# A four-layer graph network on one core: edge-feature products made a layer earlier, and a spreading one-hot moved from ScalarE to VectorE

## The chip, the core and the metric

The kernel runs on one core of a Trainium2 chip. A core has five engines with an instruction stream each: TensorE (PE, with its weight loads as PEld), VectorE (DVE), ScalarE (ACT), GpSimd (POOL) and SyncE (SP), which here only issues DMAs. Semaphores order them. Sixteen DMA engines move data between the device's memory and the on-chip SBUF; PSUM, in 8 banks, takes what TensorE computes. The metric is device time in microseconds, lower is better.

## The reference, cut to what matters

6250 nodes of 256 features, 100,000 edges sorted by destination. Four layers follow one another: attention over edges (L0), a gather-add-ReLU-sum layer (L1), a weighted graph convolution (L2), and edge attention with edge features (L3). The change touches the edge stages of the last two.

```python
# L2 (the third layer); edge_row is the source here, edge_col the destination
support = x @ W
out = segment_sum(support[edge_col] * edge_val[:, None], edge_row) + b
# L3 (the last layer), 8 heads of 32
ep = edge_features @ We + be                  # [E, 64] @ [64, 32]
scores = einsum("ehd,ehd->eh", q[dst], k[src] + ep[:, None, :]) * 32 ** -0.5
scores = scores * edge_weights[:, None]
ex = exp(scores - segment_max(scores, dst)[dst])
attn = ex / segment_sum(ex, dst)[dst]
out = segment_sum(attn[:, :, None] * v[src], dst)
```

`ep` needs only inputs of the whole kernel: no layer ahead of the last one enters it.

## The kernel before

Edges are cut into tiles of 128, and one **step** is one edge tile against one tile of 128 destination nodes. There are 832 steps, handled in **groups** of 4 (208 of them). Tables made at the start hold for each step its destination tile `j` (`k.step_j`), its edge tile `i` (`k.step_i`), and for each lane its source row, destination within the tile (`k.dloc`) and weight. All work between engines is ordered by hand: every engine runs its own loop over the groups, and the order of the calls in that loop is the engine's order.

**Third layer, `gcn_edges`.** VectorE builds for each group a one-hot of destinations (`onehot`) and a matrix `same` of lanes with the same source, times the weight. PE multiplies them (`mix_group`, L1615), ScalarE copies the result to `mix` (L1643), PE multiplies that with the tile's `support` rows (`spread_group`, L1625), ScalarE copies the sums to `update` (L1650), and GpSimd scatters them with an adding indirect DMA (L1667) into four tables, one for each step of a group. A scatter waits for the one that a group earlier went to the same table. PE and ScalarE work one group ahead with the first half (`one_ahead`). PSUM banks 0 to 5 are in use; 6 and 7 are free.

**Last layer, `att_edges`.** Four groups make a **block**; there are 52. In iteration g the engines run:

- GpSimd: gathers the keys and values of group g + 4 (L2043), multiplies 5 of 8 heads of group g - 6 with the softmax weights (L2051).
- ScalarE: `spread_group(g + 2)`: |destination - lane| (L2072), then ReLU(1 - that) (L2077), which is the one-hot that spreads queries over edges, with `first` (L2076), its first column, once a block; `part` and `mark(g - 6)`: the one-hot for summing (L2083, L2090); `weigh(g - 6)`: the other 3 heads (L2098); once a block the exponentials (L2103, L2105).
- TensorE: `look_up(g + 1)`: the edge features times `We` (L2139, into bank `EP`), the queries by the one-hot `spread` (L2145, into two banks, `LOOK`); `add_up(g - 7)`: the sums of weighted values (L2159).
- VectorE: in this order `add_features(g)`: keys plus `EP` (L2231); first of four adds to the running sums of group g - 8 (L2306); `times_query(g)` (L2237); second add; `reduce_heads(g)` (L2241); third add; fourth add.
- SyncE: loads destinations (L2004, tile `drow`) and edge features (L1999, tile `feat`) four groups ahead.

Once a block the maximum over each destination's edges is found by scans across the block: VectorE L2253 and L2258 behind `add_features` of a block's first group, PE's transposes `ends` (L2168 to L2170), VectorE L2267 and L2272, and PE's `hand_back` (L2178 to L2183); L2253 waits for a transposition of the logits (`turn`, L2164) that PE does behind `add_up` in the block's last iteration. Every buffer between PE and VectorE is single: the look-ups of g + 1 wait for `times_query(g)`, L2139 of g + 1 for `add_features(g)`, and each sum for the add of the sum before it in the same bank.

## Time and profile before

| what | us |
|---|---|
| median of 3 runs (7069.73 to 7101.26) | 7084.02 |
| the profiled execution | 7118.91 |
| its span | 7117.1 |
| scatters of the third layer, first and last start | 3173.2 to 4744.2 |
| last layer's edges, first and last `add_features` | 5002.0 to 6623.3 |

Busy over the whole span: PE 4567.6 us (64%), DVE 4218.4 (59%), POOL 4152.5 (58%), ACT 2830.5 (40%). These shares are means over stages with different limits, so they tell little about either stage. In a line of a group, "idle" is the time that the engine sat idle just ahead of that instruction, with what ended it; a semaphore number used by several stages can carry the name of another stage's DMA.

### The profile page before, as it was taken

How to read it: one execution, taken by the hardware profiler on the slowest of the kernel's cores; microseconds unless marked ns; L12 is line 12 of the kernel's file. 1: busy time of each engine (PE TensorE's matmuls, PEld its weight loads, DVE VectorE, ACT ScalarE, POOL GpSimd, SP SyncE). 2: the span in 40 equal slices, each digit the busy share in tenths (PEclk: the TensorE clock that was granted, in tenths of full speed). 3: DMA queues.
4: the chain of work that ended last, by engine and by line, in shares of the span. 5: the costliest groups of instructions: out<-in, count | busy, mean ns of one | idle time of the engine just before them, and what ended most of it. 6: DMA issues, size and time to landing. Idle time of an engine off the chain costs nothing. (4 is left out here: it accounts for less than half of the span.)

```text
span 7117.1 us, 97234 instructions
## 1 busy us (share of the span) xinstructions
PE 4567.6 (64%) x17620; PEld 3413.6 (48%) x17621; DVE 4218.4 (59%) x10350; ACT 2830.5 (40%) x7829; POOL 4152.5 (58%) x3730
## 2 busy tenths in 40 slices
PE   7366666641455544775555555547578887888799
PEld 5234333320233333464444444436466666666688
DVE  4366666676555555674444444446587877887554
ACT  0133333344333333342222222223477777777543
POOL 1666666623666666238888888851566666666210
PEclk9666676775767777897777777769788888888899
DMA  6344444424555555227777777765565555565100
GB/s 200 104 106 107 108 110 107 108 85 145 178 173 173 171 176 171 77 73 105 103 105 103 104 103 105 104 134 187 163 175 168 170 172 170 170 179 171 50 32 28
DMA packets 644440, 920.30 MB, mean 129 GB/s; under 512 B 92783, under 2 KB 500943, under 8 KB 644272
## 3 DMA queue, kind: packets, MB, share of 16 engines
q0 software_dynamic: 277808, 587.53, 36.6%
q1 hardware_dynamic: 347024, 311.25, 15.0%
q10 hardware_dynamic: 19440, 19.79, 0.8%
q14 instruction: 124, 1.02, 0.0%
q8 instruction: 44, 0.72, 0.0%
HBM read 742.43 MB, written 175.77 MB: 129 GB/s over the span
## 5 line engine op out<-in xcount | busy, mean ns | idle before, releaser
L1667 POOL DMA_INDIRECT gcn<-c_update,c_target x832 | 1319.5, 1586 | 277.3 <-issue 217.1
L1306 PE MATMUL psum<-g_rows,g_onehot 128*128 x1664 | 622.9, 523 | 765.9 <-ACT g_rows L1221 346.8
L2043 POOL DMA_INDIRECT s_rows<-kv,s_idx x832 | 798.5, 960 | 536.5 <-PE psum L2159 252.4
L662 POOL DMA_INDIRECT e_rows<-hrow,e_idx x832 | 818.3, 983 | 484.8 <-issue 234.7
L1198 POOL DMA_INDIRECT g_rows<-x,g_idx x784 | 765.4, 976 | 423.8 <-issue 229.6
L1306 PEld LDWEIGHTS psum<-g_rows,g_onehot 128*128 128x128 f32 x1664 | 387.1, 254 | 1001.7 <-issue 948.4
L725 PE MATMUL psum<-e_rows,e_onehot 128*128 128x265 f32 x1664 | 653.1, 546 | 298.7 <-DVE acc L819 116.2
L1615 PE MATMUL psum<-c_same,c_onehot 128*128 128x128 f32 x1664 | 361.5, 385 | 650.9 <-DVEq L1593 650.9
L1615 PEld LDWEIGHTS psum<-c_same,c_onehot 128*128 128x128 f32 x1664 | 307.2, 276 | 752.7 <-DVEq L1593 415.0
L725 PEld LDWEIGHTS psum<-e_rows,e_onehot 128*128 128x128 f32 x1664 | 385.8, 258 | 508.4 <-issue 213.5
L1274 DVE TENSOR_TENSOR acc<-acc,psum 128x256 f32 x832 | 349.5, 420 | 419.3 <-issue 199.7
L1625 PE MATMUL psum<-support,c_mix 128*128 x1664 | 596.4, 524 | 0.0
L2145 PE MATMUL psum<-queries_sums,s_spread 128*128 x1664 | 535.4, 478 | 92.1 <-issue 65.3
L819 DVE TENSOR_TENSOR acc<-acc,psum 128x265 f32 x832 | 357.4, 430 | 327.0 <-issue 144.5
L2098 ACT ACTIVATE s_rows<-s_rows 128x32 f32<-128x32 f32 x2496 | 549.3, 306 | 2.3
L1221 ACT ACTIVATE g_rows<-g_rows (+1 forms) x196 | 207.1, 1057 | 806.2 <-DVE g_rows L1265 471.9
L2306 DVE SCALAR_TENSOR_TENSOR queries_sums<-queries_sums,keep,psum 128x264 f32 x832 | 400.4, 481 | 153.0 <-PE psum L2159 109.4
L1598 DVE TENSOR_TENSOR c_target<-c_shift,src_f 128x4 int32<-128x4 f32 x208 | 34.0, 163 | 768.5 <-POOLq L1666 689.3
L1625 PEld LDWEIGHTS psum<-support,c_mix 128*128 128x128 f32 x1664 | 448.0, 283 | 82.9
L2145 PEld LDWEIGHTS psum<-queries_sums,s_spread 128*128 128x128 f32 x1664 | 381.4, 241 | 164.0 <-issue 101.4
L2159 PE MATMUL psum<-s_rows,s_onehot 128*128 128x264 f32 x1664 | 435.0, 407 | 9.0 <-ACT s_onehot L2090 5.8
L1643 ACT COPY c_mix<-psum 128x512 f32<-128x512 f32 x208 | 121.8, 586 | 793.1 <-PE psum L1615 790.5
(358 smaller groups left out, 9245.0 us busy)
## 6 DMA issues: line engine op xcount, KB each, us to landing
g_attr<-in_edge_attr SPq DMA_DIRECT2D x196, 512.0 KB
c_srow<-rows_src SPq DMA_DIRECT2D x208, 256.0 KB
e_drow<-rows_dloc SPq DMA_DIRECT2D x208, 128.0 KB
s_drow<-rows_dloc SPq DMA_DIRECT2D x208, 128.0 KB
s_feat<-in_edge_feat SPq DMA_DIRECT2D x832, 32.0 KB
n_sums<-gcn SPq DMA_DIRECT2D x100, 256.0 KB
e_rows<-hrow,e_idx POOLq DMA_INDIRECT x832
gcn<-c_update,c_target POOLq DMA_INDIRECT x832
```

Of the source, the lines that this page charges most:

```text
L662: pool.indirect_dma_start(rows[u][:, s, 0:D + H], None, k.hrow, bass.IndirectOffsetOnAxis(ap=idx[u][:, s:s + 1], axis=0)).then_inc(gathere ...
L725: pe.matmul(k.psum[:, s, 0:W], onehot[q % 2][:, s, :], rows[u][:, q * GROUP + s, :], start=True, stop=True).then_inc(summed, 1)
L1198: pool.indirect_dma_start(rows[:, s, :], None, k.x1, bass.IndirectOffsetOnAxis(ap=idx[:, s:s + 1], axis=0)).then_inc(gathered[n % ROUND], 16)
L1306: pe.matmul(k.psum[:, s, 0:D], onehot[q % 2][:, s, :], rows[:, bass.ds(m[q % 2 * GROUP + s], 1), :].rearrange("p o d -> p (o d)"), start=T ...
L1615: ins = pe.matmul(k.psum[:, b, s * P:(s + 1) * P], onehot[b][:, s, :], same[b][:, s, :], start=True, stop=True)
L1625: ins = pe.matmul(k.psum[:, 2 + 2 * b + s // 2, (s % 2) * D:(s % 2 + 1) * D], mix[b][:, s * P:(s + 1) * P], k.support[:, bass.ds(j[q * GRO ...
L1667: pool.indirect_dma_start(k.gcn[a], bass.IndirectOffsetOnAxis(ap=target[q][:, a:a + 1], axis=0), update[q][:, a, :], None, compute_op=ALU. ...
L2043: pool.indirect_dma_start(rows[at.u][:, st, 0:2 * D], None, k.kv, bass.IndirectOffsetOnAxis(ap=idx[at.u][:, st:st + 1], axis=0)).then_inc( ...
L2098: ins = act.activation(mine, mine, ACT.Copy, scale=rows[at.u][:, s, 2 * D + h:2 * D + h + 1])
L2145: ins = pe.matmul(k.psum[:, LOOK + s // 2, (s % 2) * D:(s % 2 + 1) * D], spread[at.b][:, s * P:(s + 1) * P], k.q[:, bass.ds(j[s], 1), :].r ...
L2159: pe.matmul(k.psum[:, s, 0:W], onehot[at.b][:, s, :], rows[at.u][:, at.q * GROUP + s, D:SLOT], start=True, stop=True).then_inc(summed, 1)
L2306: dve.scalar_tensor_tensor(out=to, in0=to, scalar=k.keep[:, bass.ds(at.g * GROUP + s, 1)], in1=k.psum[:, s, 0:W], op0=ALU.mult, op1=ALU.ad ...
```

## The change

- The edge-feature product moves into `gcn_edges`. SyncE loads the features there, 4 DMAs a group; PE multiplies them with `We` behind `mix_group`, into PSUM banks 6 and 7; ScalarE copies the 128 x 128 result out behind its copy of `mix`; SyncE stores it, 64 KB a group, to a new table `k.edge_rows` in device memory, three groups behind.
- In `att_edges` SyncE loads one 64 KB piece of that table a group in place of four feature tiles, and ScalarE copies it into PSUM bank `EP` (`move_rows`), where `add_features` reads it as before. PE's matmuls L2139 are gone.
- `spread_group` moves from ScalarE to VectorE, as one comparison of `drow` with the lane number (bf16 in, fp32 out, 512 columns), with one of a single column for `first` once a block.
- `apart` is fp32 instead of bf16; some constants and semaphores go.

```diff
@@ gcn_edges: sync @@
+            def load_feat(g, q):
+                wait_if_any(sp, rows_done, g - RING + 1)
+                i = load_indices(nc, sp, k.step_i, g * GROUP, GROUP, EA_TILES - 1)
+                for s in range(GROUP):
+                    sp.dma_start(feat[q][0:EDGE_D, s, :], edge_feat[:, bass.ds(i[s] * P, P)]
+                                 ).then_inc(feat_landed[q], 16)
+
+            def store_rows(g, q):
+                sp.wait_ge(rows_copied, g + 1 + 2)
+                sp.dma_start(k.edge_rows[bass.ds(g, 1)].rearrange("o p n -> p (o n)"), edge_rows[q][:]
+                             ).then_inc(rows_stored[q], 16)
...
+                    load_feat(g, q)
+                    if not isinstance(it, int) or q >= BEHIND:
+                        store_rows(g - BEHIND, (q - BEHIND) % RING)
@@ gcn_edges: tensor, mix_group @@
+                pe.wait_ge(feat_landed[q], (it + 1) * (16 * GROUP))
+                pe.wait_ge(rows_copied, g + 1)
+                for s in range(GROUP):
+                    ins = pe.matmul(k.psum[:, ROWS_BANK + b, s * HEAD_D:(s + 1) * HEAD_D], feat[q][:, s, :], we_sb[:],
+                                    start=True, stop=True)
+                ins.then_inc(rows_done, 1)
@@ gcn_edges: scalar, copy_mix @@
+                act.wait_ge(rows_done, g + 1)
+                wait_if_any(act, rows_stored[q], it * 16)
+                act.copy(edge_rows[q][:], k.psum[:, ROWS_BANK + b, 0:GROUP * HEAD_D]).then_inc(rows_copied, 1)
@@ att_edges: sync @@
-            def load_feat(at):
-                wait_if_any(sp, ep_done, at.g - GB + 1)
-                i = load_indices(nc, sp, k.step_i, at.g * GROUP, GROUP, EA_TILES - 1)
-                for s in range(GROUP):
-                    sp.dma_start(feat[at.q][0:EK - 1, s, :], edge_attr[:, bass.ds(i[s] * P, P)]
-                                 ).then_inc(feat_landed[at.q], 16)
+            def load_rows(at):
+                wait_if_any(sp, rows_moved, at.g - GB + 1)
+                sp.dma_start(edge_rows[at.q][:], k.edge_rows[bass.ds(at.g, 1)].rearrange("o p n -> p (o n)")
+                             ).then_inc(rows_landed[at.q], 16)
@@ att_edges: scalar @@
-            def spread_group(at):
-                act.wait_ge(drow_landed[at.q], (at.n + 1) * 16)
-                wait_if_any(act, spread_ready, at.g)
-                act.activation(off[:], drow[at.q][:], ACT.Abs, bias=minus_lane[:, 0:1]).then_inc(off_ready, 1)
-                act.wait_ge(off_ready, at.g + 1)
-                wait_if_any(act, looked_up, at.g - 1)
-                if at.q == 0:
-                    act.activation(first[at.u][:], off[:, 0:1], ACT.Relu, bias=one[:, 0:1], scale=-1.0)
-                act.activation(spread[at.b][:], off[:], ACT.Relu, bias=one[:, 0:1], scale=-1.0
-                               ).then_inc(spread_ready, 1)
+            def move_rows(at):
+                act.wait_ge(rows_landed[at.q], (at.n + 1) * 16)
+                wait_if_any(act, ep_added, at.g)
+                act.copy(k.psum[:, EP, 0:GROUP * DH], edge_rows[at.q][:]).then_inc(rows_moved, 1)
...
-                    if Group(n, q, 2).live:
-                        spread_group(Group(n, q, 2))
...
                         weigh(at)
+                    if Group(n, q, 1).live:
+                        move_rows(Group(n, q, 1))
+                    if at.live:
                         mark(at)
@@ att_edges: tensor, look_up @@
-                pe.wait_ge(feat_landed[at.q], (at.n + 1) * (16 * GROUP))
-                wait_if_any(pe, ep_added, at.g)
-                for s in range(GROUP):
-                    ins = pe.matmul(k.psum[:, EP, s * DH:(s + 1) * DH], feat[at.q][:, s, :], we_sb[:],
-                                    start=True, stop=True)
-                ins.then_inc(ep_done, 1)
@@ att_edges: vector @@
+            def spread_group(at):
+                dve.wait_ge(drow_landed[at.q], (at.n + 1) * 16)
+                wait_if_any(dve, looked_up, at.g - 1)
+                if at.q == 0:
+                    dve.tensor_scalar(first[at.u][:], drow[at.q][:, 0:1], k.lane[:, 0:1], None, ALU.is_equal)
+                dve.tensor_scalar(spread[at.b][:], drow[at.q][:], k.lane[:, 0:1], None, ALU.is_equal
+                                  ).then_inc(spread_ready, 1)
...
             def add_features(at):
                 dve.wait_ge(gathered[at.slot], (at.turn + 1) * (16 * GROUP))
-                dve.wait_ge(ep_done, at.g + 1)
+                dve.wait_ge(rows_moved, at.g + 1)
...
                     if q == GB - 1 and at.live:
                         finish_logits(at)
+                    if Group(n, q, 2).live:
+                        spread_group(Group(n, q, 2))
                     if q == 0 and done.live:
                         link_steps(done)
                     add_step(sums, 3, j)
```

VectorE's stream in `att_edges`, the end of a block's last group, before: reduction of the heads, third add, `finish_logits`, fourth add.

```order
L2241 TENSOR_REDUCE s_logit<-s_rows 128x4x8
L2303 REGISTER_ALU
L2304 REGISTER_ALU
L2306 ISA
L2306 SCALAR_TENSOR_TENSOR queries_sums<-queries_sums,keep,psum 128x264
L2247 ISA
L2247 SCALAR_TENSOR_TENSOR s_logit<-s_logit,weight 128x128
```

The same place in the changed kernel.

```order
L2269 TENSOR_REDUCE s_logit<-s_rows 128x4x8
L2331 REGISTER_ALU
L2332 REGISTER_ALU
L2334 ISA
L2334 SCALAR_TENSOR_TENSOR queries_sums<-queries_sums,keep,psum 128x264
L2275 ISA
L2275 SCALAR_TENSOR_TENSOR s_logit<-s_logit,weight 128x128
L2248 TENSOR_SCALAR s_spread<-s_drow,lane 128x512
```

The comparison stands behind the third add (in the other groups with nothing between) and ahead of the fourth.

TensorE's stream at a block's first group, before: the end transposes, then `look_up` with its feature matmuls.

```order
L2170 MATMUL psum<-s_anti,s_local 2x128
L134 ISA
L134 TENSOR_LOAD step_j
L2136 ISA
L2139 MATMUL psum<-s_we,s_feat 128x32 x4
L2142 REGISTER_ALU
L2145 ISA
L2145 MATMUL psum<-queries_sums,s_spread 128x256
```

The same place in the changed kernel.

```order
L2191 MATMUL psum<-s_anti,s_local 2x128
L135 ISA
L135 TENSOR_LOAD step_j
L2163 REGISTER_ALU
L2166 ISA
L2166 MATMUL psum<-queries_sums,s_spread 128x256
```

The four feature matmuls and the wait for them are gone from between the transposes and the look-ups.

TensorE's stream in `gcn_edges` in the changed kernel, one group (`c_onehot` by `c_same` is the mixing, `c_feat` by `c_we` the new product, `c_mix` by `support` the spreading).

```order
L1648 MATMUL psum<-c_same,c_onehot 128x128 x4
L1654 MATMUL psum<-c_we,c_feat 128x32 x4
L1661 REGISTER_ALU
L1664 ISA
L1664 MATMUL psum<-support,c_mix 128x256
```

The new product stands between the mixing of group g + 1 and the spreading of group g; all else keeps its order.

## Rows read from the trace of the kernel before

**Rows 1.** The page's first line.

```profile
span 7117.1 us, 97234 instructions
```

**Rows 2.** Busy time in a stretch of the last, then of the third layer's edges.

```profile
core 0: us, PE busy (x) PEld busy (x) DVE busy (x) ACT busy (x) POOL busy (x), PEclk, DMA share, GB/s
5400.00:6600.00 1200.00, 975.02 (x4359) 785.56 (x4359) 967.83 (x1516) 908.52 (x3110) 796.18 (x778) 0.86 0.60 172
3400.00:4600.00 1200.00, 699.22 (x2535) 558.10 (x2533) 498.08 (x2376) 253.45 (x317) 1006.96 (x635) 0.74 0.74 104
```

**Rows 3.** Third layer's scatter and update copy: count, ns least/median/most, first to last start.

```profile
L1667 POOL DMA_INDIRECT gcn<-c_update,c_target x832: 1542/1550/2071, 3173.2 to 4744.2; - x167
L1650 ACT COPY c_update<-psum x208: 1012/1012/1012, 3171.3 to 4721.8; 128x1024 f32<-128x1024 f32 x104
...
who waited for it (us, times):
  POOL gcn L1667: 3.3, 11
```

**Rows 4.** Waits from 3400 to 4600 us (the last SyncE's own): total us, times, longest.

```profile
DVE c_target L1598 <- POOLq L1666: 526.3, 139, 4.8
...
POOL gcn L1667 <- DMA gcn<-c_update,c_target: 25.6, 84, 0.3
...
SPq L1562 <- DVEq L1593: 1095.0, 158, 8.0
```

**Rows 5.** Groups by line, 5400 to 6600 us, VectorE: count | busy, mean ns | idle.

```profile
L2306 DVE SCALAR_TENSOR_TENSOR queries_sums<-queries_sums,keep,psum 128x264 f32 x622 | 299.2, 481 | 110.1 <-PE psum L2159 76.2 <-issue 13.6 <-remote 12.5
L2231 DVE TENSOR_TENSOR s_rows<-s_rows,psum 128x1024 f32<-128x1024 f32 x156 | 190.1, 1218 | 64.4 <-DMA n_x<-in_x 43.4 <-issue 10.3
L2253 DVE TENSOR_TENSOR_SCAN s_local<-s_stop,psum 128x128 f32<-128x128 f32 x39 | 16.4, 421 | 54.4 <-remote 40.6 <-DMA s_far_gap<-rows_link 8.8 <-PE psum L2164 4.1
```

**Rows 6.** The same view: the feature matmuls, and ScalarE's two passes.

```profile
L2139 PE MATMUL psum<-s_we,s_feat 65*128 65x32 f32 x1244 | 190.0, 300 | 17.3 <-DVE s_rows L2231 11.2 <-issue 5.1
L2077 ACT ACTIVATE s_spread<-s_off,s_one 128x512 f32<-128x512 bf16 x156 | 112.0, 718 | 189.3 <-PE psum L2145 133.5 <-DMA n_x<-in_x 46.9 <-ACT s_off L2072 4.9
L2072 ACT ACTIVATE s_off<-s_drow,s_minus_lane 128x512 bf16<-128x512 bf16 x155 | 110.0, 710 | 3.0 <-DMA s_drow<-rows_dloc 3.0
```

**Rows 7.** Timeline of one block: start, length, engine, line, [idle before <- releaser].

```profile
5920.85 0.42 DVE L2253 TENSOR_TENSOR_SCAN s_local<-s_stop,psum 128x128 f32<-128x128 f32 x1 [2.21 <-remote]
...
5922.69 0.48 PE L2168 MATMUL psum<-ident,s_local 128*128 128x128 f32 x1 [4.37 <-issue]
...
5924.03 1.92 PE L2139 MATMUL psum<-s_we,s_feat 65*128 65x32 f32 x8
...
5925.76 3.36 PE L2145 MATMUL psum<-queries_sums,s_spread 128*128 x8
...
5929.82 0.49 DVE L2306 SCALAR_TENSOR_TENSOR queries_sums<-queries_sums,keep,psum 128x264 f32 x1 [0.48 <-PE psum L2159]
...
5930.83 0.48 PE L2178 MATMUL psum<-s_far_gap,s_select 4*128 4x128 f32 x2
...
5932.52 1.08 PE L2139 MATMUL psum<-s_we,s_feat 65*128 65x32 f32 x8
...
5933.44 1.97 PE L2145 MATMUL psum<-queries_sums,s_spread 128*128 x8
...
5935.24 1.94 PE L2159 MATMUL psum<-s_rows,s_onehot 128*128 128x264 f32 x8
...
5937.83 0.49 DVE L2306 SCALAR_TENSOR_TENSOR queries_sums<-queries_sums,keep,psum 128x264 f32 x1 [1.86 <-PE psum L2159]
```

**Rows 8.** Comparisons and one-source passes on VectorE: ns least/median/most; last row: busy, mean.

```profile
L786 DVE TENSOR_SCALAR e_spread<-e_drow,lane x208: 327/349/593, 202.8 to 1488.5; 128x512 bf16<-128x512 bf16 x104
L952 DVE TENSOR_SCALAR n_y<-n_y,n_mv,n_std x50: 399/410/1008, 2966.0 to 3143.0; 128x256 f32<-128x256 f32 x50
L952 DVE TENSOR_SCALAR n_y<-n_x,n_mv,n_std x50: 405/410/415, 6688.9 to 7073.6; 128x256 f32<-128x256 f32 x50
...
L922 DVE TENSOR_TENSOR c_onehot<-iota,dloc 128x512 f32<-128x512 f32 x208 | 144.6, 695 | 89.6 <-DVE c_target L1598 87.6 <-issue 1.0 <-PE psum L1615 0.4
```

68 lines of the change are left out of this document (40 added, 28 removed).

## The prediction

> **What bounds the kernel now.** First comes the page for the span, 7117.1 us [rows 1], then a table of two stretches, then for each which wait ends last. The change touches two stages, and [rows 2] has a stretch of each. In the third layer's edge stage (scatters from 3173.2 to 4744.2 us [rows 3]) GpSimd is busy 1007 of 1200 us, and what is left is the 0.3 us between two scatters. VectorE waits there for GpSimd (526.3 us at L1598), SyncE for VectorE (1095 us), and GpSimd only 0.3 us at a time for a landing [rows 4]. The copy that feeds the scatters is far ahead: the last of 208 starts at 4721.8 us, the last of 832 scatters at 4744.2, so the last group's first one is at about 4738.5 (the scatters' mean spacing is 1571 / 831 = 1.89 us), some 16 us behind the copy [rows 3]; "waited for it" is 3.3 us in all. This stage is a GpSimd stage.
>
> The last edge stage (5002 to 6660 us) has no such engine. From 5400 to 6600 us PE is busy 975, VectorE 968, ScalarE 909 and GpSimd 796 us of 1200 [rows 2]: four engines at 66 to 81%, chained. 39 blocks of 4 groups pass there, one in 30.8 us, of which VectorE is idle (1200 - 968) / 39 = 5.95. Nearly all of it stands in three rows [rows 5]: 110.1 us before the adds (L2306), for PE; 64.4 before L2231; 54.4 before the first scan L2253. L2231 waits for a gather or for the feature matmuls L2139. Its "DMA n_x" is a semaphore number with another stage's name; I read it as L2139, since GpSimd runs four groups ahead. ScalarE's own idle time is mostly a wait for PE's look-ups: 189.3 us before L2077 [rows 6]. So PE and VectorE bind each other, and ScalarE is a follower.
>
> [Rows 7] walk one block, t = 0 at 5920.85, the first scan. PE does the block's end transposes at 1.84, feature matmuls at 3.18 (1.92 us long at the low clock level), look-ups at 4.91; the add of the next group starts at 8.97 after 0.48 us of waiting. Hand-back L2178 is at 9.98, features at 11.67 (1.08 us), look-ups at 12.59, their sums at 14.39, the add at 16.98 after 1.86 us of waiting. Both waits have an L2139 in the chain ahead of them.
>
> **Part by part, third layer.** PE gets 4 feature matmuls a group (8 passes): 1.08 us at the high level, 1.92 at the low [rows 7], in the same order ahead of the spreading matmuls. PE is busy 699 of 1200 us there [rows 2] at 7.55 us a group, so 1.1 to 1.9 fit, and the 16 us by which the updates end up ahead cover them. ScalarE gets one 128-column copy, under the 0.72 us of a 512-column pass [rows 6], where it is busy 253 of 1200. SyncE gets five issues a group; it idles 1095 of 1200 us. Its store waits for a copy of three groups earlier, and behind it stands the next row load, needed four groups on: hidden. DMA work moves in: 256 packets of 512 B in, 128 out a group. The last stage moves 172 GB/s at a share of 0.60; here the share is 0.74 for 104 GB/s, and 192 KB more per 7.55 us are 25 GB/s, at the last stage's ratio a share of 0.09 (estimate). At 0.83 I take no stall. Only the start shows: two feature groups ahead of the first scatter, 2 x 1.9 us at the low level plus landing: **+5 us** (0 to +15). If the cover were gone the whole 1.1 to 1.9 us a group would count, over 200 us; nothing in the rows is near that.
>
> **Part by part, last stage, per block.**
> VectorE gets 4 comparisons of 512 columns, bf16 in and fp32 out, and one of one column. No row has that form. The nearest is L786, the same comparison with bf16 out: 0.327 / 0.349 / 0.593 us (least, median, most); the other end is a 512-column pass of two fp32 inputs, 0.695 [rows 8]. I take 0.42 (nearer L786, somewhat up for the wider output), 0.2 for the single column: 1.9 us a block. The order below shows each stands between third and fourth add, behind nothing new: its look-up wait is one that L2237 has already passed.
> ScalarE loses two 0.71 us passes a group [rows 6] and gets the copy back. It was a follower: nothing by itself, but VectorE no longer depends on its arrival at PE's look-ups. Its copy waits for L2231 of the group before, and behind it stands only the one-hot of a sum one group later; L2231 has it a whole group early.
> PE loses L2139, 190.0 us in this stretch; SyncE and the DMAs lose half their bytes and 3 of 4 issues, with nobody waiting for them.
>
> The walk again, without L2139 and with the new comparison. (1) Look-ups at 3.2 instead of 4.91, the add at 8.9: VectorE arrives there 0.42 later and no longer waits, so +0 in sum (8.97 before). (2) Sums end earlier, but the fourth needs VectorE's fourth add, so hand-back is at about 8.9; look-ups then need only L2237, at 10.9 instead of 12.59. From look-up to add it was 16.98 - 12.59 = 4.4; so the add could start at 15.3. VectorE arrives at 16.98 - 1.86 + 0.42 = 15.5. **-1.5**. (3) Two comparisons and the single column until the fourth group's L2237: **+0.6**. (4) From there to the next first scan the path is PE's (look-ups, sums, transposition of the logits); VectorE waits 2.21 us before that scan [rows 7], so the fourth comparison is hidden. Sum at an unchanged clock **-0.9 us** a block. I leave the 2.1 us that lie between the end of the first sum pair (5935.24 + 0.48) and the add that waits for it (5937.83) as they are; no row explains them.
>
> Two corrections. **Port:** VectorE's one-source passes are sometimes long beside GpSimd: L952 with a median of 410 has a 1008 in one node stage and stays under 416 in the last [rows 8], L786 with 349 has a 593. GpSimd is busy two thirds of this stage. +0.1 (0 to +0.6). The Trainium skill, "SBUF — State Buffer", "Who interferes with whom", says that a tensor_scalar in a two-port mode and a GpSimd instruction exclude each other for their whole length. By it a comparison that meets L2051 could wait most of a microsecond, and the sum would be near the slower rival's; the medians of rows 8 show that most do not.
> **Clock:** PE has a granted clock of 0.86 at a busy share of 0.81, and 0.74 at 0.58 [rows 2]. Without L2139 the share is (975 - 190) / (1200 - 20) = 0.67, on the line between them 0.79; time at 1.2 GHz goes from 28 to 43%, 4.5 us more a block. At that level look-ups and sums of a group need twice 3.9 us against some 6.1 of VectorE, about 0.2 us lost per us: up to 0.8. The low stretches now lie at the block's start, where PE waits anyway; I take +0.3 (0 to 1.3).
>
> Sum: -0.9 + 0.1 + 0.3 = -0.5 us a block, 52 blocks: -26; with +5: **-21 us**. The profiled execution has 7118.9 us (span 7117.1); it comes to 7098, and the median 7084 to **7063**.
>
> **Rivals.**
> *More comes free (6980).* If VectorE alone sets the pace, a block is 24.8 busy + 1.9 + about 2 us of waits for the scans, 28.7: -2.1 x 52 + 5 = -104. For: every engine loses work but VectorE. Against: step (4) stays PE's. 0.14.
> *PE's clock takes it back (7115).* The share of 1.2 GHz becomes that of the third layer, 0.52, 7 us more a block, +1.3: -0.9 + 0.1 + 1.3 = +0.5, x 52 + 5 = +31, 7115. The Trainium skill, "TensorE: Matmul & The Clock Gate", "HAM oscillation — how this bites in real kernels", says idle gaps between bursts throw the array back to the half rate; by that rule thinning PE's work is no gain. The trace bears it out as far as the lower share goes with the lower clock in rows 2, but PE's waits in front of look-ups stay far shorter than the one in front of the end transposes. 0.15.
> *VectorE becomes the bound (7136, slower).* Place: the comparison ahead of the fourth add, three times a block on the path. If it costs 0.69 rather than 0.42 and 0.2 of port each, that is 3 x 0.47 = +1.4: -0.5 + 1.4 = +0.9, x 52 + 5 = +52. It decides from about 0.6 us each. For: no row of this form, VectorE already at 81%. Against: L786. 0.18.
> *The third layer pays.* A scatter waits for the one a group before on the same table; more packets could delay landings beyond that. 0.1 us a scatter would be +83 us, 7146. Rows 4 show no wait over 0.3. 0.04.
> *It does not do what it says:* the feature matmuls would still be on the last stage's path in another dress, as ScalarE's copy, if that came late. It would give about 7084 + 5. 0.03, inside the forecast's range.
>
> **How the numbers follow.** The forecast has 0.46, with its own range 7025 to 7100. A measurement of this kernel tells about 0.5% (35 us) from no change. Faster by more, below 7049: 0.14 and 0.20 of the forecast's. Slower by more, above 7119: 0.18, 0.04 and a little of the clock's. Rest 0.43. Range 6990 to 7130: it leaves out the ends of the first and third rival.
>
> **What would show it.** Right: no wait for PE before the addition of features to the keys; the wait before the second add of a block (1.86) nearly gone; the comparison at 0.35 to 0.45; GpSimd's spacing of 1.89 kept in the third layer; block 30.3. Wrong: a comparison over 0.6; granted clock under 0.78 in the last stage; scatters that wait for landings; or the idle before the first scan growing by what was saved.

## The result

The changed kernel took 6914.76 us, median of 5 runs (6888.0 to 6928.39), beside 7083.2 us for the kernel before in the same comparison: a ratio of 0.9756, with a 95% interval of 0.9735 to 0.9776. That is 168 us less. The forecast was 21 us less, and the lower end of its range was 6990. The sign was right, and the time lies below the range.

The profiled execution of the changed kernel has 6888.0 us (span 6886.3). Its two stretches, a table with the columns of [rows 2]:

```profile
5200.00:6400.00 1200.00, 915.50 (x3524) 684.15 (x3524) 1144.92 (x1935) 858.57 (x3300) 912.37 (x873) 0.88 0.63 182
3400.00:4600.00 1200.00, 897.11 (x3846) 760.75 (x3845) 506.07 (x2412) 297.80 (x480) 1004.78 (x642) 0.71 0.83 131
```

VectorE went from 968 to 1145 of 1200 us in the last stage: it now has 1.25 us of idle time in a block of 27.3 us, where it had 5.95 in 30.8. The groups of the same stretch answer to [rows 5] (busy, mean ns | idle time before):

```profile
L2334 DVE SCALAR_TENSOR_TENSOR queries_sums<-queries_sums,keep,psum 128x264 f32 x704 | 334.2, 475 | 36.4 <-PE psum L2180 16.2 <-issue 8.1 <-remote 5.6
L2259 DVE TENSOR_TENSOR s_rows<-s_rows,psum 128x1024 f32<-128x1024 f32 x176 | 212.5, 1207 | 8.0 <-issue 8.0
L2248 DVE TENSOR_SCALAR s_spread<-s_drow,lane 128x512 f32<-128x512 bf16 x175 | 90.7, 518 | 0.0
L2281 DVE TENSOR_TENSOR_SCAN s_local<-s_stop,psum 128x128 f32<-128x128 f32 x44 | 18.5, 420 | 10.6 <-PE psum L2185 8.2 <-issue 2.3
```

All three waits of [rows 5] are much shorter: 110.1 us in 39 blocks became 36.4 in 44, 64.4 became 8.0, and 54.4 became 10.6. The new comparison has a mean of 0.518 us. The scatters of the third layer, the comparison and the addition of features over the whole run (ns least/median/most, first to last start), against [rows 3] and, for the addition, the table of times ahead of the prediction:

```profile
L1712 POOL DMA_INDIRECT gcn<-c_update,c_target x832: 1542/1551/2063, 3150.4 to 4705.1; - x167
```

```profile
L2248 DVE TENSOR_SCALAR s_spread<-s_drow,lane x208: 464/476/1969, 4956.1 to 6389.4; 128x512 f32<-128x512 bf16 x104
```

```profile
L2259 DVE TENSOR_TENSOR s_rows<-s_rows,psum x208: 1183/1203/1223, 4963.0 to 6395.5; 128x1024 f32<-128x1024 f32 x104
```

From the first to the last scatter it is 1554.7 us instead of 1571.0, and from the first to the last addition of features 1432.5 instead of 1621.3. The pair of profiles is 230.8 us apart: 22.8 of it lie ahead of the scatters, in code that the change leaves alone, 16.3 among the scatters, 188.8 in the last stage, 3.0 behind it. The medians are 168 apart, so some 60 us are the difference of two single executions.

### The profile page after: what moved, and what is told of

Read it like the earlier page. It is cut to its first block and busy times, and to the rows that moved or that the text cites. A ratio compares the mean times of both kernels' runs of the same rounds, so it can differ in the third digit from the quotient of the medians.

```text
span 6886.3 us, 98886 instructions
## 1 busy us (share of the span) xinstructions
PE 4592.4 (67%) x17620; PEld 3430.3 (50%) x17621; DVE 4278.0 (62%) x10609; ACT 2679.4 (39%) x7777; POOL 4159.0 (60%) x3730
## 5 line engine op out<-in xcount | busy, mean ns | idle before, releaser
L1712 POOL DMA_INDIRECT gcn<-c_update,c_target x832 | 1303.3, 1566 | 271.4 <-issue 235.4
L2077 POOL DMA_INDIRECT s_rows<-kv,s_idx x832 | 817.4, 982 | 341.6 <-issue 221.7
L1664 PEld LDWEIGHTS psum<-support,c_mix 128*128 128x128 f32 x1664 | 427.3, 269 | 76.0
L676 ACT ACTIVATE e_rows<-e_rows 128x64 f32<-128x64 f32 x1664 | 407.5, 333 | 16.4 <-issue 15.4
```

What stands on the lines that cost most here:

```text
L676: ins = act.activation(rows[u][:, s, at], rows[u][:, s, at], ACT.Copy, scale=rows[u][:, s, D + h:D + h + 1])
L1664: ins = pe.matmul(k.psum[:, 2 + 2 * b + s // 2, (s % 2) * D:(s % 2 + 1) * D], mix[b][:, s * P:(s + 1) * P], k.support[:, bass.ds(j[q * GRO ...
L1712: pool.indirect_dma_start(k.gcn[a], bass.IndirectOffsetOnAxis(ap=target[q][:, a:a + 1], axis=0), update[q][:, a, :], None, compute_op=ALU. ...
L2077: pool.indirect_dma_start(rows[at.u][:, st, 0:2 * D], None, k.kv, bass.IndirectOffsetOnAxis(ap=idx[at.u][:, st:st + 1], axis=0)).then_inc( ...
```

## Two levels of one kernel

The experiments came in five sets, each with the kernel before run beside it, and the kernel before did not take the same time in all of them. It took 6558 and 6562 us in the first two sets, and 7080, 7078 and 7136 us in the three later ones; beside the result it had 7083. The text calls these the quick and the slow level. Kernels of one set share the level, so ratios are compared within a level only. The number of the chip does not tell which it is: chip 8 had both. A profile of the kernel before from the quick level shows what is different.

> The kernel before, unchanged, for its profile beside the ones of this call. The first four experiments ran on a chip on which the kernel before takes 6558 us and whose profiles have no wait named remote, while the first pair of profiles (7119 and 6888 us) had such waits, some 2 us long, around VectorE, GpSimd and ScalarE in the last stage. Theory L (signals between engines come late on the first chip): this run has a last stage of about 1450 us on such a chip and over 1600 us on one like the first. Theory N (the chips differ in DMA or clock only): the idle times of VectorE have the same causes on both, and no remote.

It took 6569.11 us, in one run. From the first to the last addition of features it needs 1470.2 us (4606.5 to 6076.7), the changed kernel beside it 1421.7. What SyncE waits for, first at the slow level (kernel before, 5200 to 6200 us; us in total, times, longest):

```profile
SPq L134 <- PE psum L2139: 53.3, 17, 4.6
SPq L134 <- DMA n_x<-in_x: 13.7, 6, 4.4
```

and then at the quick level (the same kernel, 5000 to 6000 us):

```profile
SPq L134 <- PE psum L2139: 305.6, 70, 6.3
```

SyncE, which only issues DMAs, has 67 of 1000 us to spare at the slow level and 306 at the quick one. The difference shows in its own register instructions for the feature loads, slow level first (ns least/median/most):

```profile
L1999 SPq FUSED_REGOPS  x832: 3/37/1477, 4993.2 to 6593.7; - x167
```

```profile
L1999 SPq FUSED_REGOPS  x832: 37/37/47, 4597.2 to 6042.3; - x167
```

At the slow level an instruction of 0.037 us takes up to 1.477 us at times. There, too, signals of PE come late. The timeline of the kernel before at the slow level has the product of a group on PE and the addition of features that waits for it:

```profile
5474.71 1.05 PE L2139 MATMUL psum<-s_we,s_feat 65*128 65x32 f32 x8
...
5484.32 1.22 DVE L2231 TENSOR_TENSOR s_rows<-s_rows,psum 128x1024 f32<-128x1024 f32 x1 [5.64 <-DMA n_x<-in_x]
```

The product ended at 5475.76 us, and the addition starts 8.6 us later, after 5.64 us of waiting. The keys that it also needs had landed 19 us before. ("DMA n_x" is another stage's name on the semaphore of the product, as the prediction says.) In the stretch of [rows 5] 15 of 156 of these waits are longer than 1 us. They make 41.8 of the 64.4 us, and each ends 2.4 to 8.6 us after the product's end on PE. The first scan is alike: its 16 waits named "remote" (40.6 us), a name that the profile gives where it finds no release, end 1.7 to 3.9 us after PE's transposition of the logits, and 4 us or more after the landing of the tables that it also needs. This is theory L. In the quick level's profile, from 4800 to 6000 us, no wait before the addition is over 1 us, the longest of the first scan for PE is 0.3 us, and "remote" is not there at all.

## The experiments

The ratio is to the kernel before of the same set. The changed kernel itself was not run again in the later slow sets: its 0.9756 is from the set of the result, and differences from it at the slow level go across sets.

| kernel | level | median us | ratio | 95% interval |
|---|---|---|---|---|
| changed | slow | 6914.76 | 0.9756 | 0.9735 to 0.9776 |
| changed | quick | 6501.89 | 0.9902 | 0.9885 to 0.9919 |
| features only | quick | 6496.17 | 0.9906 | 0.9889 to 0.9922 |
| features only | slow | 6911.54 | 0.9759 | 0.9742 to 0.9775 |
| spread only | quick | 6556.79 | 0.9998 | 0.9988 to 1.0008 |
| spread only | slow | 7092.45 | 1.0019 | 1.0009 to 1.0029 |
| comparison twice | quick | 6592.38 | 1.0051 | 1.0034 to 1.0068 |
| PE product back, late | quick | 6662.01 | 1.0160 | 1.0143 to 1.0177 |
| PE product back, early | quick | 6549.28 | 0.9973 | 0.9961 to 0.9984 |
| PE product back, early | slow | 7024.59 | 0.9930 | 0.9910 to 0.9949 |
| loads back on SyncE | slow | 7082.81 | 1.0011 | 1.0001 to 1.0020 |
| loads back, fixed address | slow | 6991.20 | 0.9803 | 0.9783 to 0.9824 |
| before, fixed address | slow | 7105.26 | 0.9953 | 0.9934 to 0.9971 |
| shared spread | quick | 6495.80 | 0.9897 | 0.9880 to 0.9914 |
| before, PE late | slow | 7073.59 | 0.9990 | 0.9978 to 1.0002 |
| changed, PE late | slow | 6953.44 | 0.9825 | 0.9808 to 0.9841 |
| rows from SBUF | slow | 6902.88 | 0.9751 | 0.9735 to 0.9768 |
| no GpSimd multiply | slow | 6921.05 | 0.9770 | 0.9754 to 0.9787 |

### Which of the two moves

Features only: `spread_group` goes back to ScalarE, in the two passes it had before.

```diff
-            def spread_group(at):
-                dve.wait_ge(drow_landed[at.q], (at.n + 1) * 16)
...
+            def spread_group(at):
+                act.wait_ge(drow_landed[at.q], (at.n + 1) * 16)
+                wait_if_any(act, spread_ready, at.g)
+                act.activation(off[:], drow[at.q][:], ACT.Abs, bias=minus_lane[:, 0:1]).then_inc(off_ready, 1)
...
```

> The changed kernel, but ScalarE keeps the spreading one-hot of the last layer in its two passes, at the place it had before; VectorE's comparison is gone. So of the two moves only that of the edge-feature product is made. Theory A (the move of the product off PE made the gain; the comparison is a pure cost to a VectorE that is now busy 95% of the last stage): VectorE loses 4 x 0.52 + 0.2 = 2.3 us a block, but ScalarE comes to 19.5 + 4 x 1.42 = 25.2 us a block, against 27.3 for the block now, so a block takes 25.5 to 26.5 and the time is 6830 to 6880. Theory B (the gain came from VectorE having the one-hot ready for PE, which ScalarE brought late): most of the gain goes again, time 7000 to 7080. Theory C (each half brings about half): 6970 to 7010.

> The kernel with the product's move alone (ScalarE keeps the one-hot), once more, for a call in which the kernel before takes 7080 us; where it takes 6560 this kernel was at 0.991. Theory S (with late signals the product on PE is what makes VectorE wait; taking it off gives the whole gain there too): 6900 to 6940 where the kernel before takes 7080. Theory T (with late signals each engine that PE depends on costs, and a one-hot from ScalarE is one more handoff): 6980 to 7040. Where the kernel before takes 6560: 6490 to 6500 again.

Spread only: the kernel before with VectorE's `spread_group`, and no other edit.

> The kernel before, with the spreading one-hot of the last layer made on VectorE as in the changed kernel; the edge features are still multiplied in the last layer by PE. Theory A (the product's move made the gain): VectorE has 2.3 us more a block while its 5.9 us of waits for PE stay in part; between +0 and +2.3 us a block, 7083 to 7200. Theory B (the one-hot from VectorE made the gain): 6920 to 6990. Theory C (half each): 6990 to 7030.

> The kernel with the one-hot's move alone (the product stays in the last layer), once more. Theory S: 7050 to 7090 where the kernel before takes 7080. Theory T (the handoff from ScalarE is what late signals lengthen): 6970 to 7040. Where the kernel before takes 6560: 6550 to 6560 again.

At both levels the features' move has the whole gain (0.9906 and 0.9759, beside 0.9902 and 0.9756 for both moves), and the one-hot's move has none: 0.9998 and 1.0019. (Features only keeps the changed kernel's fp32 `apart`, which was not run alone.) The time of 6496 us is no gain of 35 to 85 us over the changed kernel, as theory A wanted for a VectorE freed of 2.3 us a block. A shorter wait alone says little, too: in the slow profile of spread only, VectorE's wait before the addition of features is 6.7 us in 1000, where the kernel before has 44.1 in the same stretch, though the product is still on PE; the wait for PE's sums is 113.4 instead of 94.1, and the time does not fall. Theories B and C fall, and so does T at the slow level.

> The changed kernel, unchanged, beside the experiments. Theory A (VectorE bounds the last stage after the change, each 0.52 us comparison counts in full): the run with each comparison twice took 6592, less 4 x 0.48 x 52 = 100 is 6492, a ratio of 0.990 to the kernel before, and the features-only kernel (6496) is no worse. Theory R (the gain is a fixed share): 0.9756 x 6558 = 6398. Theory L in addition: on a chip with late signals the ratio is about 0.976, without them about 0.99.

The changed kernel was at 6502 at the quick level, near the 6492 worked out from the comparison made twice. So the change is worth 60 us there and 168 at the slow level: a share R it is not.

### Is VectorE the bound, and is PE

Comparison twice:

```diff
+                dve.tensor_scalar(twice[at.b][:], drow[at.q][:], k.lane[:, 0:1], None, ALU.is_equal)
                 dve.tensor_scalar(spread[at.b][:], drow[at.q][:], k.lane[:, 0:1], None, ALU.is_equal
```

> The changed kernel with each 512-column comparison made twice, first into a scratch tile, then as before. If VectorE is the bound of the last stage (theory A and B alike): 4 x 0.52 = 2.1 us a block, 52 blocks, +108 us, 7000 to 7025. If the last stage is bound elsewhere and VectorE's 95% are filled with waits that look like work: under +30 us, 6915 to 6945.

Against the changed kernel at this level it is (1.0051 - 0.9902) x 6560 = 98 us for 208 more comparisons, close to the 108. More VectorE work counts in full. Less of it does not:

> The changed kernel with the spreading one-hots of the last layer shared: VectorE makes those of even groups (and the single column), ScalarE in two passes those of odd groups. VectorE loses 2 x 0.48 = 1.0 us a block against the changed kernel, ScalarE gains 2 x 1.42 = 2.8 and is at 22.4 us a block of about 26. If VectorE bounds the last stage: -1.0 x 52, some 40 to 50 us faster than the changed kernel. If PE and its clock bound it with VectorE: 0 to 20 us faster. If the mixed source of one-hots delays PE's look-ups in odd groups (as in the kernel before): 10 to 40 us slower.

```diff
+            def spread_group(at):
+                if at.q % 2 == 0:
+                    return
+                act.wait_ge(drow_landed[at.q], (at.n + 1) * 16)
...
-                pe.wait_ge(spread_ready, at.g + 1)
+                pe.wait_ge(spread_act if at.q % 2 else spread_ready, turns(at))
```

It has 0.9897, the changed kernel 0.9902: the intervals overlap. VectorE's busy time did not fall (1162 of 1200 us, 4800 to 6000, beside 1161 in the changed kernel), though it makes half as many of the comparisons. Those that it makes became longer: 87 of them have a mean of 1.052 us, and in the changed kernel 174 have 0.574 in the same stretch; the median is under 0.48 in both. The rescaling went from 0.825 to 1.316 us in the mean and the second scan from 1.461 to 0.632. So what ScalarE took over came back as longer passes of VectorE, and ScalarE, busy 946 of 1200 us, was not the limit. Part of VectorE's busy time is waiting for GpSimd, as a run further down shows; that this is what came back was not tested. With features only, ScalarE is busy 1065 of 1200 us and VectorE 1118 (4800 to 6000 us, columns of [rows 2]):

```profile
4800.00:6000.00 1200.00, 889.92 (x3531) 670.40 (x3531) 1117.59 (x1722) 1065.27 (x3702) 900.10 (x877) 0.90 0.63 184
```

There the two stand close together, and which of them holds the block was not tested.

PE's product was given back in two places, with the same matmuls on constant tiles. Late, behind the wait for the multiplication by the queries:

```diff
                 wait_if_any(pe, dotted, at.g)
+                for s in range(GROUP):
+                    pe.matmul(k.psum[:, LOOK, s * DH:(s + 1) * DH], stand_in[:, s, :], we_sb[:], start=True, stop=True)
```

> The changed kernel with four matmuls of the product's size (65 rows, 32 columns) given back to PE in each group of the last layer, on constant tiles, written to the look-up's bank right behind the wait for it and overwritten by it; nobody waits for them. It separates PE's load from the wait of VectorE for the product. If PE's load as such made the kernel before slow: 1.1 to 1.9 us a group on PE's path, over 4 us a block at worst, back to 7020 to 7100. If it was the wait of the addition of features for PE (the handoff): PE has 27 - 21 = 6 us of idle time a block and hides nearly all of it, 6915 to 6960.

Early, where the kernel before has it, with ScalarE's copy waiting for it:

```diff
+                wait_if_any(pe, ep_added, at.g)
+                for s in range(GROUP):
+                    ins = pe.matmul(k.psum[:, EP, s * DH:(s + 1) * DH], stand_in[:, s, :], we_sb[:],
+                                    start=True, stop=True)
+                ins.then_inc(ep_done, 1)
                 pe.wait_ge(spread_ready, at.g + 1)
                 wait_if_any(pe, dotted, at.g)
```

> The changed kernel with a product of the same size given back to PE in the last layer, on constant tiles, where the kernel before has it: ahead of the look-ups, behind the wait for the addition of features; ScalarE's copy of the real values waits for it and overwrites it. The run with the product behind the wait for the multiplication took 6662, over 100 us more than the kernel before. Theory P (PE's time between that wait and the look-ups is on the path, time ahead of it mostly free): 6500 to 6560, near the kernel before at most. Theory Q (any PE work of that size costs that much, by load or by clock): 6640 to 6690.

Late it costs (1.0160 - 0.9902) x 6560 = 169 us, 0.81 us a group, and early 47 us, 0.22 a group. The product takes PE nearly the same time in both (1.22 and 1.15 us a group, 4800 to 6000 us). About two thirds of it count where it stands between the multiplication and the sums, and less than a fifth ahead of that; the time there is mostly free. The kernel before has the product in the cheap place.

### SyncE

> The changed kernel with the four feature loads of a group, and the reading of their indices, given back to SyncE in the last layer, into tiles that nobody reads. It puts back what the change takes from SyncE and the DMAs of that stage, and nothing of PE. If SyncE and its loads have no part in the gain: 0 to 10 us over the changed kernel (ratio 0.976 where the kernel before takes 7080, 0.990 where it takes 6560). If on the chip of 7080 us the gain comes from SyncE's stream (its register instructions take 0.7 us at times there, against 0.03): 6980 to 7080 there, and no difference where the kernel before takes 6560.

```diff
+            def load_feat(at):
+                wait_if_any(sp, rows_moved, at.g - GB + 1)
+                wait_if_any(sp, feat_landed[at.q % 2], (at.n * 2 + at.q // 2) * (16 * GROUP))
+                i = load_indices(nc, sp, k.step_i, at.g * GROUP, GROUP, EA_TILES - 1)
+                for s in range(GROUP):
+                    sp.dma_start(feat[at.q % 2][:, s, :], edge_attr[:, bass.ds(i[s] * P, P)]
+                                 ).then_inc(feat_landed[at.q % 2], 16)
...
                         load_dst(ahead)
+                        load_feat(ahead)
                         load_rows(ahead)
```

It took 7082.81 us, 1.0011 of the kernel before, 3 us above the top of what was expected: with loads that nobody reads, and with PE's product still gone, the whole 168 us are lost again. All that SyncE waits for in this kernel from 5200 to 6200 us is one line (1.4 us in all), and what VectorE then waits for is a table that SyncE loads:

```profile
SPq L135 <- ACT psum L2121: 1.4, 1, 1.4
```

```profile
L2295 DVE TENSOR_TENSOR_SCAN s_local<-s_stop,psum 128x128 f32<-128x128 f32 x32 | 13.5, 422 | 122.2 <-DMA s_far_gap<-rows_link 90.6 <-remote 25.4 <-issue 4.6
```

SyncE is the bound of this kernel, at 31.6 us a block (1635.8 us from the first to the last addition of features, over 51.75 blocks). L2295 is the first scan, which needs the tables of segment ends. SyncE's loop here also waits for its own feature loads to land, and no such wait shows. With the stored rows SyncE has six loads a group here, the kernel before five, so this run loads SyncE more than the kernel before did. Is it the bytes or SyncE's instructions? The same loads from constant addresses have no index reads and no address arithmetic:

```diff
-                i = load_indices(nc, sp, k.step_i, at.g * GROUP, GROUP, EA_TILES - 1)
                 for s in range(GROUP):
-                    sp.dma_start(feat[at.q % 2][:, s, :], edge_attr[:, bass.ds(i[s] * P, P)]
+                    sp.dma_start(feat[at.q % 2][:, s, :], edge_attr[:, (at.q * GROUP + s) * P:(at.q * GROUP + s + 1) * P]
```

> As the run with the loads given back to SyncE (which took 7083 beside 7078 for the kernel before), but their addresses are constants: the same DMAs and bytes, without the reading of indices and the address arithmetic on SyncE. What it loads is read by nobody. If SyncE's instruction stream is the bound there (its register instructions at 0.7 us): where the kernel before takes 7080, half or more of the 168 us come back, 6915 to 6990, and SyncE shows waits again. If it is the DMA traffic or the issues themselves: 7050 to 7090. Where the kernel before takes 6560: 0.990 to 0.993 of it by either theory.

The ratio goes from 1.0011 to 0.9803 (in another set of runs), which is 82% of the way to 0.9756, and SyncE waits again (5200 to 6200 us):

```profile
SPq L2044 <- DVE s_spread L2261: 81.2, 19, 5.6
SPq L107 <- ACT psum L2120: 44.3, 28, 1.7
```

The number of loads and their bytes are the same. So most of the cost was in SyncE's instruction stream. One rival is left: the constant addresses read the same 16 tiles over and over, and no run tells whether the memory serves these sooner. The same edit in the kernel before (its last layer then uses the features of the wrong edges):

> The kernel before, whose SyncE loads the edge features of the last layer from constant addresses instead of those of each step (the features are then the wrong edges', all else is kept); TensorE's product stays. SyncE alone is relieved. By SyncE's stream as a bound of the kernel before (it waits only 68 of 1000 us in the slower condition, 306 in the quicker): where the kernel before takes 7080, down to 7000 to 7040, near the run with the product on PE but without the loads (7025). If PE's product alone is what binds it: 7065 to 7090. Where the kernel before takes 6560: no change, 6550 to 6565.

It has 0.9953, a gain of 33 us, less than the 40 to 80 expected. SyncE has 258 us to spare there, and VectorE's wait for PE's sums is even longer (111.2 in 1000 us; the kernel before has 94.1 in the same stretch):

```profile
L2305 DVE SCALAR_TENSOR_TENSOR queries_sums<-queries_sums,keep,psum 128x264 f32 x528 | 254.0, 481 | 111.2 <-PE psum L2158 79.6 <-remote 14.9 <-issue 10.7
```

> The changed kernel with a product of the same size given back to PE early, on constant tiles, under ScalarE's copy, once more. Theory S: 7020 to 7080 where the kernel before takes 7080, since the product is then on PE's path again. If it is SyncE's loads that late signals act on, and not PE's product: 6915 to 6950. Where the kernel before takes 6560: 6549 again.

With SyncE unloaded and the product on PE it is 0.993. So the 168 us of the slow level split in two: 50 with the product still on PE (the third layer's gain among them), and 123 for taking it off. SyncE has room in both of the kernels that the 123 us lie between: it waits 390 of 1000 us with the product and 362 without (5200 to 6200 us). The same step is worth 47 us at the quick level, where the product makes most of the gain: 0.9973 with it, 0.9902 without. What the slow level has in addition are PE's late signals, and without the product VectorE waits for fewer of them. That this makes the difference of 76 us fits the waits shown above; no run separates it from PE's work.

Was SyncE a limit of the kernel before? In its trace nobody waits for a feature load from 5100 to 6620 us, and from 5200 to 6400 us the last load of each group is issued 9.5 us or more before its product starts. What is waited for are the tables before the first scan (8.8 us in [rows 5]) and the destinations of the one-hots (3.0 in [rows 6]), and taking SyncE's index reads away brought 33 us. But SyncE becomes the bound when a block gets short. An estimate: it does not wait in 933 of 1000 us, which is 29.2 us of a block of 31.3 (1621.3 over 51.75), and the changed kernel's block is 27.7 (1432.5 over 51.75). The run between, the product gone and SyncE loaded just as before, was not made; by the estimate it could bring at most 2.1 of the 3.6 us a block. So at the slow level SyncE's relief is a condition of the gain more than its source.

### Late PE, GpSimd's share, the copy into PSUM

Four more matmuls once a block ahead of the sums of its second group, in either kernel:

```diff
+                    if at.q == 1 and s == 0:
+                        for _ in range(GROUP):
+                            pe.matmul(k.psum[:, 0, 0:W], onehot[at.b][:, 0, :], rows[at.u][:, at.q * GROUP, D:SLOT],
+                                      start=True, stop=True)
```

> The kernel before with four more 264-column matmuls on TensorE once a block, ahead of the sums of a block's second group and overwritten by them: PE's sums, and what follows them, come some 2.0 us (high clock level) to 3.5 us (low) later once a block. It is a stand-in for the profiles of the first chip, where about a fifth of PE's sums are signalled 1 to 3 us after their end. Theory F (VectorE of the kernel before runs into every such delay, in the changed kernel it is ahead of PE no longer and the delay is absorbed): +1.5 to 3 us a block, +80 to 150 us over the kernel before. If the kernel before absorbs it as well: under +50.

> The same four matmuls once a block in the changed kernel. Theory F: absorbed for the most part, under +0.8 us a block, +0 to 40 us over the changed kernel (0.990 of the kernel before without them), so that the difference between the two kernels grows from 60 to over 100 us. Against it stands the run with a product behind the wait for the multiplication, which cost 0.77 us a group: by that one this run costs +1 to 2 us a block, +50 to 100, and the difference stays near 60.

Theory F falls, and the other way round: the kernel before hides the delay (0.999), and the changed kernel pays (0.9825 - 0.9756) x 7080 = 49 us, 0.9 us a block. So the changed kernel has PE's chain close to the path at that place. Why the kernel before hides four matmuls there stays open: its VectorE waits longer for the sums (137.9 us in 1000 instead of 94.1), and the time is not longer.

GpSimd's multiplication of five heads left out (their sums are then unweighted):

```diff
-                pool.tensor_tensor(mine, mine, w.unsqueeze(3).to_broadcast([P, GROUP, ON_POOL, DH]), ALU.mult
-                                   ).then_inc(pool_weighed, 1)
+                pool.sem_inc(pool_weighed, 1)
```

> The changed kernel with GpSimd's multiplication of five heads by the softmax weights left out (the sums of these heads are then unweighted); its signal is kept. If VectorE's long passes (the second scan has a mean of 1.46 us where its shortest are 0.42, the rescaling 0.83 against 0.40, the comparison 0.57 against 0.47) are waits for GpSimd that count as busy time: they fall to 0.42, 0.40 and 0.48, VectorE has some 1.8 us a block less and the time is 6400 to 6440. If they have another cause: they stay, and the time is within 20 us of the changed kernel.

The second scan and the rescaling of the changed kernel at the slow level (5200 to 6400 us), then the first scan and the same two lines of this run (5200 to 6200 us):

```profile
L2286 DVE TENSOR_TENSOR_SCAN s_local<-s_stop,s_local 128x128 f32<-128x128 f32 x44 | 49.8, 1132 | 0.0
L2322 DVE TENSOR_TENSOR queries_sums<-queries_sums,s_scale 128x256 f32 x44 | 20.2, 459 | 0.0
```

```profile
L2278 DVE TENSOR_TENSOR_SCAN s_local<-s_stop,psum 128x128 f32<-128x128 f32 x36 | 15.2, 421 | 47.5 <-remote 43.1 <-issue 2.7 <-PE psum L2182 1.6
L2283 DVE TENSOR_TENSOR_SCAN s_local<-s_stop,s_local 128x128 f32<-128x128 f32 x36 | 15.0, 418 | 0.0
L2319 DVE TENSOR_TENSOR queries_sums<-queries_sums,s_scale 128x256 f32 x36 | 14.5, 402 | 0.0
```

The passes fall to 0.418 and 0.402 us, as the theory said: a part of VectorE's busy time was waiting for GpSimd. The time doesn't follow: 0.9770, not under the changed kernel's 0.9756. At the slow level what is saved comes back as idle time, 47.5 us before the first scan. At the quick level, where the changed kernel has means of 1.461 and 0.825 us, it was not run. The Trainium skill, "SBUF — State Buffer", "🔬 SBUF: two separate sides", says that whichever of the two starts first, GpSimd or a VectorE instruction with two inputs in SBUF beside a GpSimd one that reads SBUF, has the shared pair of ports for its whole length, and the other is blocked; these rows agree for the scan and the rescaling.

VectorE reads the edge rows from SBUF, without ScalarE's copy into PSUM:

```diff
-                dve.wait_ge(rows_moved, at.g + 1)
+                dve.wait_ge(rows_landed[at.q], (at.n + 1) * 16)
...
-                ep = k.psum[:, EP, 0:GROUP * DH].rearrange("p (s c) -> p s c", s=GROUP)
+                ep = edge_rows[at.q][:].rearrange("p (s c) -> p s c", s=GROUP)
```

> The changed kernel without ScalarE's copy into PSUM: VectorE's addition of features reads the stored rows where the DMA puts them, in SBUF. If the copy only costs (ScalarE has one pass less a group and nobody waits): 0 to 20 us faster than the changed kernel. If VectorE's pass with two sources in SBUF is slower than one with a source in PSUM, or shares a port with GpSimd: each of 208 passes up to 1 us longer, 6540 to 6700.

```profile
L2250 DVE TENSOR_TENSOR s_rows<-s_rows,s_edge_rows x208: 1187/1206/2200, 4962.9 to 6410.5; 128x1024 f32<-128x1024 f32 x104
```

The pass has a median of 1.206 us, as with a source in PSUM (1.203), and the ratio is 0.9751. So in time the copy costs nothing here and buys nothing. It does change something beside this pass. In 5200 to 6200 us a copy of eight columns has a mean of 1.608 us, where the changed kernel (L2290) has 0.494 at the same level, and GpSimd's gathers have 1.134 instead of 0.985. VectorE is busy 979 of 1000 us, beside 956, and waits less for the sums (11.6 us, beside 30.7). Why the two cancel was not tested. No version that was run beats the changed kernel by more than its interval.

## Why the prediction was wrong

**The step that failed** is the walk through one block, which gave -0.9 us for the last stage. Of VectorE's three waits for PE in [rows 5] it counted only the one before the second add. It left the 64.4 us before L2231 (1.65 us a block) out of the sum, and its step (4) kept the wait before the first scan, because "from there to the next first scan the path is PE's". Measured, per block: the wait before the adds went from 2.8 to 0.8 us, before L2231 from 1.65 to 0.2, before the first scan from 1.4 to 0.2. VectorE's idle time fell by 4.7 us and its work grew by 1.2, and so a block went from 30.8 to 27.3 us. Behind these waits stands what the prediction took for PE's work: at the slow level two of the three are in good part PE's signals that come late. The rows showed it (1.65 us a block, and "remote" before the scan), but a walk through one block, without such a wait before L2231, did not.

At the quick level, from profile to profile, the last stage lost 1470.2 - 1421.7 = 48.5 us, 0.94 a block. The walk's -0.9 is that number, but by luck: the comparisons cost more than it took, and waits that it left out went. What separates 0.94 from the forecast's 0.5 are the terms for clock and port, +0.3 and +0.1; the third layer, below, is the rest of the miss at that level.

**SyncE** was put at nothing: it and the DMAs "lose half their bytes and 3 of 4 issues, with nobody waiting for them". That nobody waited is nearly right for the kernel before. But a queue that waits only 67 of 1000 us is nearer to its limit than any engine of [rows 2], and a block of 27 us is not to be had with it: the loads' return, beside the new load, took back the whole 168 us, their return without index reads 33 of it. The prediction's rows show SyncE's waits for the third layer (1095 of 1200 us, [rows 4]) and not those of the last one.

**The clock** did not fall. PE's busy share in the last stage went from 0.81 to 0.76 and the granted clock from 0.86 to 0.88; at the quick level the share went from 0.86 to 0.75 with the clock at 0.88 both times (5000 to 6000 us). The line through two stages that gave 0.79 was no law. The +0.3 of the sum has nothing to stand on, and the rival of 7115 fell with it. The rule on idle gaps of the Trainium skill, "TensorE: Matmul & The Clock Gate", "HAM oscillation — how this bites in real kernels", cited there, is not borne out by these two pairs. The run with the loads back agrees with it: PE waits up to 10.6 us before the end transposes, where the changed kernel has 4.1, and the clock is 0.84 beside 0.89 (5200 to 6200 us).

**The comparison** was taken at 0.42 and has a median of 0.476 and a mean of 0.518; with the single column at 0.20 it adds 2.3 us a block, and the forecast had 1.9 and 0.1 for the port. The third rival's picture of VectorE as the bound fits its 1145 of 1200 us, but the block became shorter and not longer. The comparison twice showed the price of one more in full, 98 us for 208. The one-hot's move, taken alone, brings nothing at either level.

**The third layer** was given +5 us. It gained: 1571.0 to 1554.7 us among the scatters in this pair, 1578.9 to 1555.4 at the quick level, and between 1552 and 1558 in every profile with the product there. The pages of the two profiles say where: the gaps between scatters are nearly the same (277.3 and 271.4 us in all), and the scatters themselves are 20 ns shorter in the mean (1.586 and 1.566 us). Why was not tested. What was right there: the product, its copy, the loads and the stores at a DMA share of 0.83, against 0.74 in [rows 2], are hidden behind GpSimd.

**The rivals.** "More comes free" (6980) was the right kind, and too small: it priced a block at 28.7 us, and it was 27.3 in the stretch above. It had 0.14. Its argument, that every engine loses work but VectorE, was near to what happened, and step (4), put against it, was wrong.

## What to carry to other kernels

Go through all waits of the bounding engines by their totals before a walk through one block decides which of them count. Before a change that takes DMAs or index reads off a queue is priced at nothing, ask how long that queue waits in the stage at hand; a queue has no busy column in the tables, and its idle time is the only number that tells how near it is. Where several engines stand at 80%, two limits can hide each other: taking away one can be worth little, and the sum of single edits says little about both. And an addition to an engine's work costs by its place in the order more than by its length: the same four matmuls cost 0.22 us a group ahead of the wait and 0.81 behind it.

## What was not expected of the hardware

- One kernel has two levels, 6560 and 7080 to 7136 us, on a chip of the same number. At the slow one SyncE's register instructions take up to 1.4 us instead of 0.04, and VectorE, waiting for PE, starts 2 to 8 us after the end of PE's work at times. What sets the level stays open; loads back and fixed addresses were measured at the slow level alone.
- The granted clock of PE did not fall with less work on it: 0.86 to 0.88 for a busy share of 0.81 and 0.76, and 0.88 twice for 0.86 and 0.75. It was 0.84 at a share of 0.68 in the run with the loads back.
- VectorE passes with all operands in SBUF can show as busy while they wait for GpSimd: 1.13 us in the mean for a scan that takes 0.418 when GpSimd's multiplication is gone.
- A 1024-column addition of VectorE has a median of 1.206 us with its second source in SBUF and 1.203 with it in PSUM, but other passes, and GpSimd's gathers, became longer beside the first.
